# Exponent arguments of a state-space scan for both directions in one instruction, one group ahead

## The reference, cut to what matters

```python
delta = jax.nn.softplus(dt @ dt_w.T + dt_b)
A = -jnp.exp(A_log)
dA = jnp.exp(delta[..., None] * A)
dBu = delta[..., None] * Bm[:, :, None, :] * xc[..., None]

def step(h, inp):
    da, dbu, c = inp
    h = da * h + dbu
    return (h, jnp.einsum('bdn,bn->bd', h, c))
h0 = jnp.zeros((B, delta.shape[-1], n), x.dtype)
_, ys = jax.lax.scan(step, h0, (dA.swapaxes(0, 1), dBu.swapaxes(0, 1), Cm.swapaxes(0, 1)))
```

## Time and profile before

| what | value |
|---|---|
| runs of the kernel before | 547.98, 547.00, 543.64 us, median 547.0 us |
| the profiled execution | 538.17 us, its span 536.4 us |
| TensorE (PE) busy | 488.0 us, 91% of the span |
| VectorE (DVE) busy | 377.9 us, 70% |
| ScalarE (ACT) busy | 239.7 us, 45% |
| GpSimd (POOL) busy | 169.4 us, 32% |
| mean granted clock of TensorE | 0.959 of full speed |
| spread-delta matmuls, L1515 | 128, mean 400 ns |
| arguments on VectorE, L1711 | 128, mean 686 ns |
| exponentials on ScalarE, L1617 | 128, mean 626 ns |

### The profile page before, as it was taken

The page is one execution under the profiler, slowest core; times in us unless marked ns, Lnnn a source line. Parts: engine busy times, 40 slices in busy tenths (PEclk is TensorE's granted clock), DMA queues, the critical chain, the costliest instruction groups (busy, mean ns, idle before and its releaser), DMA issues. The chain is left out here.

```text
span 536.4 us, 6835 instructions
## 1 busy us (share of the span) xinstructions
PE 488.0 (91%) x1812; PEld 239.5 (45%) x1812; DVE 377.9 (70%) x718; ACT 239.7 (45%) x416; POOL 169.4 (32%) x159
## 2 busy tenths in 40 slices
PE   6989999999999998998887958989999998989997
PEld 3535555655555475544543512222222222376553
DVE  0066576566576676644898769999999999277755
ACT  1112213113212211759978547788878888121100
POOL 6000100100100112221221016898888889242000
PEclk9999999999999999997587959999999999999999
DMA  9981009200000000400246565575657555300000
GB/s 271 308 261 38 1 15 322 82 1 1 1 1 0 0 1 5 144 0 28 70 121 174 142 187 158 161 196 146 168 144 202 146 166 164 111 4 12 10 11 20
DMA packets 36426, 53.55 MB, mean 100 GB/s; under 512 B 5652, under 2 KB 27184, under 8 KB 36402
## 3 DMA queue, kind: packets, MB, share of 16 engines
q1 hardware_dynamic: 35746, 52.52, 33.8%
q10 hardware_dynamic: 656, 0.73, 0.4%
HBM read 35.83 MB, written 17.27 MB: 99 GB/s over the span
## 5 line engine op out<-in xcount | busy, mean ns | idle before, releaser
L1681 POOL TENSOR_TENSOR gb<-da,hb 128x512 f32<-128x512 f32 x94 | 116.9, 1277 | 57.6 <-ACT da L1617 57.6
L1711 DVE TENSOR_TENSOR da<-ps,expA 128x512 f32<-128x512 f32 x128 | 85.0, 686 | 6.7 <-PE ps L1515 5.5
L304 PE MATMUL ps<-xbuf,convw 128*128 128x384 f32 (+1 forms) x240 | 82.8, 498 | 4.5 <-DMA convw<-in_conv_wT 4.5
L1617 ACT ACTIVATE da<-da 128x512 f32<-128x512 f32 x128 | 78.0, 626 | 15.7 <-DVE da L1711 13.3
L358 PE MATMUL ps<-wall,peT 128*128 128x512 f32 x144 | 67.8, 593 | 0.0
L304 PEld LDWEIGHTS ps<-xbuf,convw 128*128 128x128 f32 (+1 forms) x240 | 46.0, 195 | 36.3 <-ACTq L501 4.1
L1515 PE MATMUL ps<-drows,selb 96*128 96x512 bf16 x128 | 50.5, 400 | 12.4 <-DMA drows<-dparts 6.7
L1527 PE MATMUL ps<-urows,brows 96*128 96x512 bf16 x128 | 48.7, 398 | 1.4 <-DVE gb L1718 0.8
L528 ACT ACTIVATE kvs<-ps 128x512 f32<-128x512 f32 x36 | 21.5, 597 | 57.4 <-PE ps L358 57.4
L520 ACT ACTIVATE peT<-ps 128x384 f32<-128x384 f32 x24 | 11.8, 490 | 75.0 <-PE ps L304 75.0
L1729 DVE TENSOR_TENSOR hb<-gb,ps 128x512 f32<-128x512 f32 x64 | 42.1, 679 | 0.0
(11 more groups left out here) (216 smaller groups left out, 746.6 us busy)
## 6 DMA issues: line engine op xcount, KB each, us to landing
xbuf<-in_xT SPq DMA_DIRECT2D x11, 768.0 KB
yscr<-yst SPq DMA_DIRECT2D x30, 208.0 KB
brows<-bparts SPq DMA_DIRECT2D x16, 240.0 KB, 3.4
uparts<-pt SPq DMA_DIRECT2D x24, 128.0 KB, 2.4
dparts<-pt SPq DMA_DIRECT2D x24, 128.0 KB, 2.4
drows<-dparts SPq DMA_DIRECT2D x15, 192.0 KB, 2.7
urows<-uparts SPq DMA_DIRECT2D x15, 192.0 KB, 3.2
inw<-in_in_wT SPq DMA_DIRECT2D x2, 1024.0 KB
```

The costliest lines, as they stand in the source:

```text
L304: mm = pe.matmul(bank(T_EMB + j % 2, 0, EN), convw[0:n, k, h * P:(h + 1) * P], xbuf[0:n, q, k, c * EN:(c + 1) * EN], start=(k == 0), stop= ...
L1617: act.activation(da_at(q, j), da_at(q, j), ACT.Exp, scale=-1.0).then_inc(da_ready, 1)
L1681: pool.tensor_tensor(gb_at(q, j), da_at(q, j), hb[:, s_ - 2, d, :], ALU.mult).then_inc({2: m2_done, 3: m3_done, 4: m4_done}[s_], 1)
L1711: dve.tensor_tensor(da_at(q, j), bank(j % 2), expA[:, j % 2, :], ALU.mult).then_inc(e_free, 1)
```

## The change

Everything is float32 as before and the same values are computed.

- The two directions of a step go together. TensorE does two matmuls, one into bank 0 and one into bank 1, and raises `e_ready` once, after the second. One VectorE instruction of 128x1024 reads both banks, and raises `e_free` once. One ScalarE instruction of 128x1024 takes both exponentials. So there are 64 of each where there were 128.
- Before, bank 0 could be refilled while VectorE read bank 1. Now both are released together by one instruction.
- The arguments and exponentials of a group are computed one group earlier than half of them were: all four pairs of group g+1 are made while the states of group g are summed. A second set of decay tiles, `da1`, holds them. `yst` and `margin` move or grow in memory, and the expert weights take the memory of `inw`, the input projection, which is no longer needed then.
- SyncE loads the delta rows of group g+2 as before, but those of u and B behind the store of group g's first outputs.
- The order on every engine but GpSimd is rewritten to fit.

The diff, cut to its core:

```diff
+        expw = inw[:, :, :, :].rearrange("p d h n -> p d (h n)")
...
+        da1 = sb("da1", [P, 4, DI], ctx=scn)
...
-        def da_at(q, j):
-            return da[:, j + (2 if j >= 6 and q == 1 else 0), :]
+        def da_at(q, j, n=1):
+            if j >= 2 and q == 1:
+                return da1[:, j - 2:j - 2 + n, :] if j < 6 else da[:, j + 2:j + 2 + n, :]
+            return da[:, j:j + n, :]
...
-                        sp.wait_ge(e_ready, 8 * g + 8)
-                        load_rows(sp, g + 2, q)
+                        sp.wait_ge(e_ready, 4 * g + 4)
+                        load_delta(sp, g + 2, q, 0, ST)
...
+                    if not last:
+                        load_u(sp, g + 2, q, 0, ST)
+                        load_b(sp, g + 2, q)
...
-            def spread_delta(g, q, j):
-                o = (j // 2) * DI
-                pe.wait_ge(e_free, 8 * g + j + 1)
-                pe.matmul(bank(j % 2), selb[:, j % 2, :], drows[:, q, o:o + DI],
-                          start=True, stop=True).then_inc(e_ready, 1)
+            def spread_pair(g, q, s_):
+                pe.wait_ge(e_free, 4 * g + s_ + 1)
+                for d in range(2):
+                    mm = pe.matmul(bank(d), selb[:, d, :], drows[:, q, s_ * DI:(s_ + 1) * DI], start=True, stop=True)
+                mm.then_inc(e_ready, 1)
...
-                act.activation(da_at(q, j), da_at(q, j), ACT.Exp, scale=-1.0).then_inc(da_ready, 1)
+                act.activation(da_at(q, 2 * s_, 2), da_at(q, 2 * s_, 2), ACT.Exp, scale=-1.0).then_inc(da_ready, 1)
...
-                dve.tensor_tensor(da_at(q, j), bank(j % 2), expA[:, j % 2, :], ALU.mult).then_inc(e_free, 1)
+                dve.tensor_tensor(da_at(q, 2 * s_, 2), ps[:, 0:1024].rearrange("p (d n) -> p d n", d=2), expA[:, :, :],
+                                  ALU.mult).then_inc(e_free, 1)
...
-                    argument(g, q, 4)
-                    argument(g, q, 5)
-                    argument(g, q, 6)
+                    if after:
+                        arguments(g + 1, 1 - q, 0)
                     state(g, q, 2, 0)
-                    argument(g, q, 7)
+                    if after:
+                        arguments(g + 1, 1 - q, 1)
                     state(g, q, 2, 1)
                     if after:
-                        for j in range(3):
-                            argument(g + 1, 1 - q, j)
-                        for d in range(2):
-                            decayed_1(g + 1, 1 - q, d)
-                        argument(g + 1, 1 - q, 3)
+                        arguments(g + 1, 1 - q, 2)
+                        decayed_1(g + 1, 1 - q, 0)
+                        decayed_1(g + 1, 1 - q, 1)
+                        arguments(g + 1, 1 - q, 3)
                         for d in range(2):
                             state(g + 1, 1 - q, 1, d)
```

More of the change, by code:

```diff
@@ L1242, in prepare_vector @@
             ch = Chain(dve, x_chain)
-            dve.sem_inc(e_free, 2)
+            dve.sem_inc(e_free, 1)
             dve.sem_inc(bu_used, 2)
@@ L1555, in scan_tensor @@
             pe.wait_ge(skip_ready, NI - 1)
-            for j in range(4):
-                spread_delta(0, 0, j)
+            for s_ in range(2):
+                spread_pair(0, 0, s_)
             pe.wait_ge(u_landed[0], 16 * 4)
             pe.wait_ge(skip_ready, NI)
-            for j in range(4):
+            for j in range(2):
                 b_times_u(0, 0, j)
             pe.wait_ge(d_landed[0], 16 * 2)
-            for j in range(4, 6):
-                spread_delta(0, 0, j)
+            spread_pair(0, 0, 2)
+            for j in range(2, 4):
+                b_times_u(0, 0, j)
+            spread_pair(0, 0, 3)
+            pe.wait_ge(d_landed[1], 16)
+            spread_pair(1, 1, 0)
             def body(i, first, last):
@@ L1594, in body @@
                     if after:
-                        spread_delta(g + 1, 1 - q, 4)
                         b_times_u(g + 1, 1 - q, 2)
                         b_times_u(g + 1, 1 - q, 3)
+                    if not last:
+                        pe.wait_ge(d_landed[q], 16 * i + (48 if q == 0 else 32))
+                        spread_pair(g + 2, q, 0)
                     add_decayed(g, q, 0)
-                    if after:
-                        spread_delta(g + 1, 1 - q, 5)
             def keep_clock(n):
@@ L1633, in copy_state @@
                 act.activation(hb[:, 2, d, :], bank(4 + d), ACT.Copy).then_inc(h3_copied, 1)
-            for j in range(4):
-                exponential(0, 0, j)
+            for s_ in range(4):
+                exponentials(0, 0, s_)
             def body(i, first, last):
@@ L1641, in body @@
                     after = not (last and q == 1)
+                    if after:
+                        exponentials(g + 1, 1 - q, 0)
                     if not (first and q == 0):
                         copy_state(g - 1, 1)
-                    exponential(g, q, 4)
-                    exponential(g, q, 5)
                     stage_c(g, q)
-                    exponential(g, q, 6)
-                    exponential(g, q, 7)
+                    if after:
+                        exponentials(g + 1, 1 - q, 1)
                     copy_y(g, 0)
                     if after:
-                        for j in range(3):
-                            exponential(g + 1, 1 - q, j)
+                        exponentials(g + 1, 1 - q, 2)
+                        exponentials(g + 1, 1 - q, 3)
                     if not (first and q == 0):
@@ L1701, in scan_vector, with arguments @@
             dve.wait_ge(skip_ready, NI)
-            def argument(g, q, j):
-                dve.wait_ge(e_ready, 8 * g + j + 1)
-                if j in (2, 3):
-                    need(dve, m2_done, 2 * g + j - 3)
-                elif j in (4, 5):
-                    need(dve, m3_done, 2 * g + j - 5)
-                elif j >= 6:
-                    need(dve, m4_done, 2 * g + j - 9)
-                dve.tensor_tensor(da_at(q, j), bank(j % 2), expA[:, j % 2, :], ALU.mult).then_inc(e_free, 1)
+            def arguments(g, q, s_):
+                dve.wait_ge(e_ready, 4 * g + s_ + 1)
+                if s_ == 0:
+                    need(dve, bu_used, 2 + 6 * g - 4 if isinstance(g, int) and g == 0 else 6 * g - 2)
+                else:
+                    need(dve, (m2_done, m3_done, m4_done)[s_ - 1], 2 * g - 2)
+                dve.tensor_tensor(da_at(q, 2 * s_, 2), ps[:, 0:1024].rearrange("p (d n) -> p d n", d=2), expA[:, :, :],
+                                  ALU.mult).then_inc(e_free, 1)
             def decayed_1(g, q, d):
-                dve.wait_ge(da_ready, 8 * g + d + 1)
+                dve.wait_ge(da_ready, 4 * g + 1)
                 if d == 0:
@@ L1730, in state @@
                                   ALU.add).then_inc(bu_used, 1)
-            for j in range(3):
-                argument(0, 0, j)
+            for s_ in range(3):
+                arguments(0, 0, s_)
             decayed_1(0, 0, 0)
             decayed_1(0, 0, 1)
-            argument(0, 0, 3)
+            arguments(0, 0, 3)
             for d in range(2):
```

36 lines of the change are left out of this document (13 added, 23 removed).

## The result

The changed kernel took 553.78, 552.83, 551.16 and 552.67 us, median 552.75 us; the kernel before, measured with it, 545.32 us. The ratio of the two is 1.0194, its 95% interval 1.0136 to 1.0251. It is slower. The forecast was 553.0 us, from a base of 547.0 and a shift of +6.1. By the medians the shift is +7.4, by the ratio 10.6. The profiled execution of the changed kernel took 553.78 us, its span is 552.0. So what lies ahead of the scan moves from run to run, and I compare inside the scan.

A forecast was written before the change was run, and what follows sets the result against it. VectorE was taken to bound the loop. Without waits -4.7 us, loop waits +8.1, beginning +1.6 and +1.1 gave +6.1 on 547.0: 553.0 us, bounds 550.8 to 556.9, with a wider range of 545 to 559.

The forecast's parts named there:

- The tail: End of the scan, GpSimd's last six multiplies and the multiply after: unchanged in length, shifting as S15 shifts.
- S15: Mark where the scan's end begins, group 15's first state: forecast 456.5 us against 450.42, bounds 454.2 to 460.3.
- A wide argument: VectorE's 128x1024 instruction: record about 1.22 us, costing 1.14 where two narrow ones cost 1.20.
- The second and third waits of a group: VectorE in the loop: 0.19 us before argument pair 2, 0.12 before the next group's first decay.
- The beginning's arguments: First wide arguments after the second delta load: pair 2 at 320.02 us, pair 3 at 324.0; 1.6 us lost.
- S0: Mark at the first state of group 0, after argument pair 3: forecast at 325.1 us.
- argument pair 0 to pair 1: VectorE in each group: natural distance 1.74 us, possible 2.01 after the bank refill, so a wait of 0.27.
- the 1.1 us of waits in group 0: Group 0 at the beginning: VectorE's waits taken as 1.1 us, between 0.58 at full and 1.7 at half clock.
- the forecast's bound for the half clock: Group 0 with TensorE at half clock: waits of 1.7 us, a pair taking 1.14 to answer.
- S1: Mark at group 1's first state: forecast 334.3 us, bounds 333.7 to 335.0, against 327.65; 6.65 later.
- The second rival: TensorE becomes the bound: outputs lag 0.3 us more each group, S15 +13.4 us, time 560; chance 0.13.
- The fast rival: Wide operations pay: refill hidden in the loop, 545.0 us, or 542.3 with the beginning hidden too; chance 0.17.

The follow-up runs named there:

- e_swap: Changed kernel with TensorE's add_decayed(g, 0) put ahead of the wait for the next group's first pair; 548.40 us, ratio 1.0168 to the kernel before.
- e_fill: e_clock with four more extra matmuls in TensorE's holes of group 0, results unused; 552.08 us, ratio 1.0183 to the kernel before.
- c_before: The kernel before, unchanged, run again for a second trace; 542.30 us, ratio 1.0007.
- e_start: Changed kernel with the beginning's order of before: decays and step-1 states of group 0 ahead of the second load's wait; 551.93 us, ratio 1.0191.
- e_best_b2: e_best_b with three extra TensorE matmuls ahead of the second delta load, results unused; 536.42 us, ratio 0.9890 to the kernel before.
- e_clock: Changed kernel with five extra identity matmuls on TensorE ahead of the second delta load, results unused; 555.47 us, ratio 1.0234 to the kernel before.
- e_best_b: Kernel before with spread 6 ahead of a step-3 B-times-u on TensorE and stage_c ahead of exponentials 4 and 5 on ScalarE; 536.36 us, ratio 0.9881.

## Why the forecast was right, and what it mis-sized

**What held.** The tail moves with S15: 8.21 us behind it, as forecast. A wide argument is 1.22 long with a step of 1.14 and saves 0.06. The 0.125 us that the Trainium skill (Perfetto Trace Analysis, Optimizing Scalar/DVE Operations) gives for a VectorE instruction's overhead on PSUM is not there; the measurement decides. The second and third waits of a group, 0.19 and 0.12 forecast, are 0.18 and 0.16 (0.25 in two groups). The beginning's arguments came at 1.07 and 5.05 us as worked out, S0 at 6.19 against 6.15.

**First mis-sized term: argument pair 0 to pair 1, 0.27.** It is 0.54. The step took TensorE to be free when the argument ends, and left out its in-order queue: two fp32 identity sums of 0.86 us and two B-times-u stand behind pair 0. This is 0.27 a group, 3.8 us. e_swap takes it out and leaves the forecast's 0.28; its group of 8.79 is 0.06 above the forecast's 8.73.

**Second mis-sized term: the 1.1 us of waits in group 0.** It was a middle between 0.58 at the full and 1.7 at the half clock. The half clock stayed nearly to the end of group 0, and the waits are 2.6 us: 10.79 us instead of 9.2, 1.6 more. So the forecast's bound for the half clock was too low as well, by 0.9 us; half of the waits is the 1.33 us before the decays, which wait for a B times u queued behind pair 2 and the outputs. At the full clock 0.58 was right: group 0 of e_fill takes 8.77 us, of which 0.62 is waiting. (By the same terms the lower bound of S1 should be 333.8, not 333.7; nothing hangs on it.)

**The sum.** S1 is 8.3 us later than in the first trace of before (6.65 forecast), and fourteen groups take 126.5 us instead of 122.8 (122.2 forecast). That is +12.0 us, against the +6.1 of the forecast; against c_before it is +9.7. The second rival (outputs lagging, S15 at +13.4) had the size almost, but not the place: it put the lag at the outputs, and TensorE held up the second pair. Set on the marks of the first trace, S15 comes at 462.4 us, past the forecast's upper bound of 460.3; the +9.7 against c_before would put it at 460.1, just inside. That the measured 552.75 us meets 553.0 so closely is luck: the base was 547.0 in the forecast, while the kernel before gave 542 to 545 us later, and this made up for the shift forecast too small. The sign and mechanism were right; the shift was about 60% of what the ratio shows, and 80% of the medians' 7.4.

**The fast rival** needed less than 0.34 us of new waits a group; there are 0.88 to 0.96.

**Left open.** S1 is 8.3 us later, of which e_start accounts for 1.6 us by the order of the beginning and e_fill for 2.0 by the clock; most of the rest the forecast put down to work that is done ahead, and no run takes that apart. No run moves the u and B loads alone; in the changed kernel's trace no wait of an engine between the second load and S15 is ended by a landing. Nor does a run narrow the exponentials; none of VectorE's three waits of a group is ended by ScalarE. Why the clock fell behind S15 in e_start and in e_best_b2 (0.57 from 457 to 461 us), and not in the changed kernel, is not shown.

## What to carry to other kernels

An instruction that joins two buffers also joins their release. Price it as end of the instruction, refill, and start of the next, and read the producer's queue ahead of the refill, where one fp32 matmul took as long as four bf16 ones; against that stood 0.06 us saved per joined pair. An order that computes a stage further ahead pays at the beginning, where the first group has nothing to overlap with, and gets nothing back if the end hangs on another chain. Before widening anything, look for the short waits of the saturated engine: here two moved lines gave 0.27 us a group.

## What the runs showed of the hardware

- An fp32 identity matmul of 128x512 holds TensorE 0.86 us at the full clock, four times a bf16 one's 0.22. VectorE starts 0.42 us after the start of the matmul that it waits for (324.23 to 324.65 in the earlier trace rows), and 0.50 after it where a register operation stands between (382.44 to 382.94 in the earlier trace rows).
- In e_clock the clock was 1.00 from 323 to 326 us, behind the extra matmuls, and 0.59 from 326 to 330 us, behind a stretch in which TensorE was busy 1.09 of 3 us. The half clock can return inside a group: c_before and e_clock each lost 1.7 us in one group for it. Behind S15 it came with 1.45 us more to the next multiply in e_start (9.66 against 8.21).
- What lies ahead of the scan differed by 3.5 us between e_best_b and e_best_b2, whose code there is the same (first spread at 311.9 and 315.5 us), and by up to 4.4 over all traces.
